# Reordering VectorE's first operations in a two-layer transformer kernel: rope products of the first batch together, statistics of a later batch behind them

## The reference

```python
x = x + L0_attn(layernorm(x), Wq, Wk, Wv, Wo, gate_w)   # 16 heads of 8, rope on Q and K, causal, two softmaxes
x = x + L0_ffn(layernorm(x), W1, b1, W2, b2)            # relu, 512 wide
x = x + L1_attn(layernorm(x), ln_g, ln_b, Wq, bq, ...)  # 16 heads of 8, not causal
x = x + L1_ffn(layernorm(x), w_gate, w_up, w_down)      # silu gate, 384 wide, integer weights
```

```python
Q = rope(heads(Wq)); K = rope(heads(Wk)); V = heads(Wv)     # heads(W) = (xn @ W.T) split into 16 heads
s = (Q K^T + 0.1 * (Q*Q) (K*K)^T) / sqrt(8)                 # causal mask, softmax, times V
out2 = attend(rotate_half(Q), rotate_half(K))               # a second attention on the rotated halves
```

## Time and profile before

| | before |
|---|---|
| median of 3 runs | 309.39 us |
| lowest, highest | 309.39, 310.2 us |
| the profiled execution's own time | 311.73 us |
| its span | 310.0 us |
| mean granted TensorE clock | 0.983 of full |
| PE busy | 288.1 us, 93% |
| DVE busy | 246.9 us, 80% |
| ACT busy | 213.2 us, 69% |
| POOL busy | 182.2 us, 59% |

### The profile page before, as it was taken

One profiled execution on the slowest core, in us unless ns is written; L12 is line 12 of the kernel. 1 busy time (PEld: TensorE's weight loads), 2 busy tenths in 40 slices (PEclk: granted clock), 3 DMA queues, 4 the chain that ended last, 5 costly groups with the idle time before them and its releaser, 6 DMA issues.

```text
span 310.0 us, 8437 instructions
## 1 busy us (share of the span) xinstructions
PE 288.1 (93%) x2833; PEld 206.1 (66%) x2833; DVE 246.9 (80%) x992; ACT 213.2 (69%) x494; POOL 182.2 (59%) x409
## 2 busy tenths in 40 slices
PE   6498898899998999999999999999999999999985
PEld 4375555677676777878687776766666666666564
DVE  7669987687869877686878777679898989896764
ACT  8463784776576868685867768697778767677921
POOL 5475879887785878687778514525455535353210
PEclk9967999999999999999999999999999999999999
DMA  6477436511313121221212010021211101000001
GB/s 188 151 196 176 110 94 178 163 51 56 121 39 103 36 85 54 80 59 41 76 39 60 21 57 26 28 62 29 60 45 52 53 28 44 28 22 1 20 18 35
DMA packets 23691, 21.60 MB, mean 70 GB/s; under 512 B 3712, under 2 KB 20608, under 8 KB 23648
## 3 DMA queue, kind: packets, MB, share of 16 engines
q1 hardware_dynamic: 23648, 21.05, 23.5%
HBM read 13.18 MB, written 7.34 MB: 66 GB/s over the span
## 4 chain that ended last, share of the span: by engine, by line
PE 50%; DVE 22%; POOL 16%; issue 5%; ACT 3%; DMA 2%; SPq 1%; POOLq 0%; ACTq 0%; DVEq 0%
PE bank L1000 11%; DVE NM L779 7%; PE bank L974 5%; PE bank L1043 4%; PE bank L1030 4%; PE bank L950 4%; POOL PB L489 3%; PE bank L951 3%; PE bank L978 3%; POOL XN L443 3%; DVE JUNK L776 3%; PE bank L1089 3%; POOL RS L439 2%; POOL PR L459 2%; DMA xs<-in_x 2%
## 5 line engine op out<-in xcount | busy, mean ns | idle before, releaser
L615 ACT ACTIVATE PB<-bank 128x384 f32<-128x384 f32 (+1 forms) x256 | 134.3, 545 | 47.1 <-PE bank L976 23.6
L779 DVE TENSOR_REDUCE NM<-bank 128x2 f32<-128x512 f32 x128 | 83.8, 683 | 19.7 <-PE bank L951 19.4
L974 PE MATMUL bank<-QS,KS 128*128 128x256 f16 x256 | 69.9, 274 | 3.8 <-ACT PB L615 2.6
L1000 PE MATMUL bank<-PB,VP 128*32 128x256 f32 (+1 forms) x1024 | 61.7, 358 | 0.4 <-ACT PB L615 0.4
L776 DVE CUSTOM_DVE_ANT_0 JUNK<-bank,MSF 128x256 bf16<-128x256 f32 x128 | 53.7, 419 | 0.0
L774 DVE CUSTOM_DVE_ANT_0 JUNK<-bank,MSF 128x128 bf16<-128x128 f32 x128 | 36.3, 284 | 19.5 <-PE bank L948 19.0
L1000 PEld LDWEIGHTS bank<-PB,VP 128*32 128x32 f32 x1024 | 26.8, 109 | 23.2 <-issue 9.7
L489 POOL TENSOR_SCALAR_AFFINE_SELECT PB<-PB 128x512 f32<-128x512 f32 x64 | 41.2, 643 | 0.0
L950 PE MATMUL bank<-KS,QS 96*128 96x256 f16 x128 | 35.2, 275 | 0.4
L948 PE MATMUL bank<-KS,QS 96*128 96x256 f16 x128 | 34.9, 275 | 0.0
L951 PE MATMUL bank<-KS,QS 96*128 96x256 f16 x128 | 34.6, 271 | 0.0
(11 more groups left out here) (104 smaller groups left out, 590.7 us busy)
## 6 DMA issues: line engine op xcount, KB each, us to landing
scr<-PR SPq DMA_DIRECT2D x16, 256.0 KB, 2.6
QS<-scr SPq DMA_DIRECT2D x16, 128.0 KB, 2.6
QS<-scr SPq DMA_DIRECT2D x32, 64.0 KB, 2.8
KS<-scr SPq DMA_DIRECT2D x32, 64.0 KB, 2.7
KS<-scr SPq DMA_DIRECT2D x16, 128.0 KB, 2.9
scr<-PR SPq DMA_DIRECT2D x16, 128.0 KB, 1.9
out_x<-xs SPq DMA_DIRECT2D x8, 128.0 KB, 2.0
W<-in_w SPq DMA_DIRECT2D x1, 576.0 KB, 4.8
```

The lines of the kernel that those rows point to most:

```text
L615: act.activation(PB[:, s % RING, 0:n], scored(i, s)[:, 0:n], ACT.Exp).then_inc(s_e, 1)
L779: dve.tensor_reduce(m[:, s, 0:2], o[:, :].rearrange("q (n k) -> q n k", n=2), AX.X, ALU.max, negate=True).then_inc(s_mx, 1)
L974: pe.matmul(o[:, 0:S], k[:, 0:P], q[:, :], start=True, stop=True)
L1000: ins = pe.matmul(o, v, pr, start=(g % 2 == 0 and kt == 0), stop=True, skip_group_check=True)
```

## The change

Only the order of VectorE's calls in the prologue is changed. No operation is added or removed, and no other engine's list differs.

```diff
             product(0, 0)
+            product(0, 1)
             dve.wait_ge(s_x[2], 16)
             variance(0, 2)
-            product(0, 1)
             low(0, 0)
+            low(0, 1)
             product(1, 0)
-            low(0, 1)
+            product(1, 1)
             normalise(2)
-            product(1, 1)
-            variance(0, 3)
             low(1, 0)
             low(1, 1)
+            variance(0, 3)
             for n in range(2):
                 product(2, n)
```

## The result

| | before | changed |
|---|---|---|
| median, beside each other | 309.92 us (6 runs) | 312.6 us (6 runs) |
| lowest, highest | 309.39, 310.77 | 311.8, 312.86 |
| ratio, with 95% interval | | 1.0078 [1.0059, 1.0097] |
| the profiled execution's own time, and span | 311.73, 310.0 | 312.86, 311.0 |

The change makes the kernel slower by 0.8%, 2.5 to 2.7 us, where 0.3 us less was forecast. The forecast was 309.1 us, with a range from 308.2 to 310.2. The two spans differ by only 1.0 us, because the profiled execution of before took 1.8 us more than the median of its kernel (311.73 against 309.92).

The account below looks back on a forecast made before the run. Bound: a chain half TensorE, then VectorE and GpSimd, 2% DMA, so a prologue shift reaches the end. Terms -1.28 + 0.72, +0.62 through ScalarE, -0.34 by GpSimd gave -0.3 us: 309.1 us, range 308.2 to 310.2.

Parts of the forecast that it names:

- step 1: VectorE's queue, prologue front: a product fits into the idle wait for rows, so batch 2's normalisation starts 1.28 us earlier.
- step 3: Batch 3's statistics moved late: through GpSimd and ScalarE's fills, costs 1.16 us on ScalarE, leaving 0.06 us lost.
- step 4: Into phase 0: GpSimd's rope sums, then batch 3's lows and the cuts come earlier; 0.3 us is left.
- Step 2: Batch 2's normalisation on VectorE collides with GpSimd's rope sums: 0.72 us taken back, transposes 0.56 us earlier.
- rival (b): TensorE's clock stays up or comes back sooner, shortening batch 3's projections: -1.0 us, 308.4; 10%.
- (c): GpSimd holds batch 2's rope sums longer, behind norm(0, 3): 1.46 us more on ScalarE's copy, 310.5; 15%.
- (a): No collision at batch 2's normalisation, or both instructions ahead of the rope sum: front 1.0 to 1.1 us earlier, 308.3; 20%.
- (d): Nothing arrives: a wait in phases 0 to 4 not set by this prologue swallows it, 309.4; 10%.

Follow-up runs that it names:

- full fills: Small matmuls on idle TensorE through the whole prologue and over phase 0's first heads: before 309.52 us, again 310.15; changed kernel 310.77 us.
- the first set of fills: Small matmuls on TensorE behind heads 3 to 9 only: changed kernel 310.69 us, kernel before 310.97 us.
- the second set: Small matmuls on TensorE ahead of batch 2's transposes and the first scores, and behind heads 0 to 9: before 310.24 us, changed kernel 311.77 us.

## Why the prediction was wrong

Three terms failed: the gain of 1.28 us of step 1, the price of step 3, and in step 4 the durations of batch 3's projections. The first cut came 2.7 us later than in a usual execution of before (35.97 against 33.23), where the sum had it 0.3 us earlier.

**Its frame.** It saw that the profiled execution lay 2.34 us over the median and took that as an offset to subtract. It was not one. The two largest waits that steps 1 and 2 rest on belong to executions that start late: statistics of batch 2 at 10.26 us behind a wait of 1.37 for the rows, and a normalisation that therefore stood at 14.88. In the profiles of kernels with before's front and early statistics in which batch 2's statistics started by 9.32, it stands at 12.9 to 13.2; in the two with full fills, where they started at 9.89 and 9.99, at 13.78 and 14.30.

**Step 1** failed as a gain. The times that it forecast for the new order hold within 0.3 us (low pair 11.08 and 12.05, forecast 10.92 and 11.80; normalisation 13.86, forecast 13.60). But the 1.28 us was the distance to 14.88. With rows landing in time for statistics at 9.0 to 9.3, product(0, 1) ahead of the statistics delays them to 9.59, and two products ahead of the normalisation delay that to 13.60 against 12.89 in before with fills, or 13.21 in its second profile. The term is +0.4 to +0.7 us, not -1.28.

**Step 2** had the collision right for the new order, with its size a quarter too large: the pair took 1.05 us, forecast 1.31, against 0.60 in the orders that avoid GpSimd's rope sums (12.40 us, full fills). The transposes came at 14.97, the very number, and that was luck: the pair began 0.26 us later than forecast and was 0.26 us shorter. As a difference it was wrong: in a usual execution the old order collides too (1.00 us at 13.21), so the change takes nothing back. The rule of the Trainium skill, "SBUF — State Buffer", section "Who interferes with whom", agrees with these three pairs, in that VectorE lost time only beside GpSimd's rope sums.

**Step 3** had the chain right, link by link: high(2, 1) at 23.57 (forecast 23.70), copy at 26.25 without idle time (26.48), projections at 26.77 (26.98). Its price was 0.06 us, because the copy stood at 26.26 in the profile of before. It stands at 24.31 in the second one, so the change costs 1.9 us at the copy and 1.8 at the projections, of which the late statistics alone make 1.5 (with fills, 25.89 against 24.38). The experiment with the late statistics alone shows the cause, and the one with the copy between the fills that ScalarE's queue is a link. One link was missed: norm(0, 4), which the prediction left among what does not hang on the copy, stands behind GpSimd's work on `VP`, and so behind the same fills. With full fills on TensorE that is what sets the cut.

**Step 4** took project(3, 0) and (3, 1) at the durations of before, 1.69 and 1.03 us. They took 2.04 and 1.91, and product(3, 1) slid to 30.88 (forecast 29.86), the lows to 33.48 (forecast 32.4). That is the clock, which the prediction had only as a gain, in rival (b). The rope sum rotate(3, 0) stood at 29.63, as forecast to the hundredth, but by luck: GpSimd was ready at 29.30 and waited for the product. The fills take 1.7 us off the changed kernel (312.51 to 310.77), far beyond its spread. Off before they take 0.5 (310.05, of its runs on the same chip, to 309.52) or 0.1 (310.26 to 310.15, on another), neither clear of noise. So of the 2.5 us between the medians an estimated 1.2 to 1.6 is the clock's, and 0.9 to 1.3 stays at full clock; the first cuts with fills, 1.34 us apart, agree with the upper end of that.

**Rivals.** (c), slower through norm(0, 3) ahead of the rope sums of batch 2, named the place and the sign, but priced it by stretched GpSimd instructions that did not occur (XN took 0.88 us). (a) did not happen. (b) half happened: in the first profile of the changed kernel the clock stayed up behind the idle stretch of 3.10 us, in the second, behind 3.23 us, it was at half from 14.2 to 17.8, and neither changed the time, since the later stretch over batch 3's projections stayed. (d) fell for the kernels without fills: from the first cut on the shift is kept to 0.2 us.

## What to carry to other kernels

When the profiled execution is slower than the median by more than the effect you forecast, find out which of its waits are its own, with a second profile, before pricing anything against it (here that was worth 2 us at one copy); idle time for a transfer at the start is the first suspect. In queues served in order, an operation moved behind others must be priced at every engine that has something queued behind its consumer (here statistics, GpSimd's rope sums, ScalarE's fills, and behind these both TensorE's projections and GpSimd's work on `VP`), and against the shortest slack seen, not the slack of one trace. And where TensorE waits longer than before ahead of large matmuls, price them at half clock too.

## What the runs showed of the hardware

- The same 256 KB of rows, issued at 3.7 us, let the statistics start behind a wait for them at 9.13, 9.32, 9.89 and 10.26 us in profiles whose engines' lists are equal up to there. This is a spread of 1.1 us that orders with work in that gap do not show.
- The granted clock fell to half without a long idle stretch right ahead of it: in the changed kernel TensorE was busy 0.32 of 2 us in 18 to 20, then 1.26 and 1.08 of 2 us, at clock 1.00, and was at 0.50 in 24 to 26 us. It came back only at 30.8 us, though it was busy all of 28 to 30. In the two profiles of the changed kernel the half clock lasted from 24.0 to 30.8 and from 24.5 to 31.3 us, and in the one with only the statistics late from 25.4 to 32.2.
- Small matmuls in TensorE's idle time cost nothing measurable here (before with full fills 0.9987 and 0.9994 of before, both intervals with 1 in them), but in the two kernels with the first set of fills a half-clock stretch came at 30.2 or 32.3 us, behind the last of them. In the changed kernel with the second set it cost 1.0 us, where it fell on the first exponentials.
- VectorE's `z` (line 825 with full fills), with two inputs in SBUF, took 0.42 or 0.43 us in two profiles and 0.97 or 0.98 in 18. GpSimd's cut, begun 0.06 or 0.07 us behind it, took 0.85 or 0.86 us in those two and 0.63 to 0.65 in the others. So one of the two lost time in every profile, and what decided which of them is open.
